# Gathering by addition: P's rows are added onto scattered Q rows in SBUF, and the identity product goes

## The reference

```python
msg_in = jnp.concatenate([x[src], x[dst], edge_attr], axis=-1)
msgs = jnp.maximum(msg_in @ mW1 + mb1, 0.0) @ mW2 + mb2
agg = jax.ops.segment_sum(msgs, dst, num_segments=num_nodes)
```

## Time and profile before

| | |
|---|---|
| median of 3 runs | 910.36 us (910.34 to 913.0) |
| the profiled execution's own time | 917.49 us |
| its span | 915.6 us |
| TensorE busy | 833.4 us (91%) |
| DVE / ACT / POOL busy | 633.4 / 506.6 / 507.5 us |
| mean granted TensorE clock | 0.968 |

### The profile page before, as it was taken

The page is one execution under the profiler, slowest core; times in us unless marked ns, Lnnn a source line. Parts: engine busy times, 40 slices in busy tenths (PEclk is TensorE's granted clock), DMA queues, the critical chain, the costliest instruction groups (busy, mean ns, idle before and its releaser), DMA issues.

```text
span 915.6 us, 18961 instructions
## 1 busy us (share of the span) xinstructions
PE 833.4 (91%) x6949; PEld 777.7 (85%) x6949; DVE 633.4 (69%) x1769; ACT 506.6 (55%) x1006; POOL 507.5 (55%) x495
## 2 busy tenths in 40 slices
PE   5448888798999989999999998999999999999996
PEld 4348878798998989998899998978899888898886
DVE  7449999688798887897978888548742311127663
ACT  5226656575786777786777876634344011114864
POOL 8577777777777777777777777661210000005110
PEclk9769999999999999999999999999999999999999
DMA  6524545867565655565555655482147777686501
GB/s 175 165 80 130 155 157 170 151 200 240 170 206 161 190 167 173 166 204 177 180 172 164 206 179 169 148 258 84 45 180 306 293 298 291 239 293 203 155 24 28
DMA packets 104976, 163.68 MB, mean 179 GB/s; under 512 B 14698, under 2 KB 65425, under 8 KB 104878
## 3 DMA queue, kind: packets, MB, share of 16 engines
q1 hardware_dynamic: 91230, 134.19, 44.5%
q0 software_dynamic: 13648, 28.21, 12.1%
HBM read 107.92 MB, written 54.43 MB: 177 GB/s over the span
## 4 chain that ended last, share of the span: by engine, by line
PE 43%; POOL 37%; issue 11%; DMA 4%; DVE 3%; ACT 1%; SPq 1%; DVEq 0%; POOLq 0%
POOL room L816 36%; PE ps L1971 14%; PE ps L1956 13%; PE ps L1796 3%; DMA room<-p_rows,idx 2%; PE ps L1797 2%; PE ps L1810 2%; PE ps L1940 2%; PE ps L1827 2%; PE ps L1829 2%; PE ps L1731 1%; POOL pair L816 1%; DMA ST<-in_src 0%; ACT h L917 0%; DVE nb L1213 0%
## 5 line engine op out<-in xcount | busy, mean ns | idle before, releaser
L816 POOL DMA_INDIRECT room<-p_rows,idx x416 | 426.5, 1025 | 132.7 <-issue 125.6
L1796 PE MATMUL ps<-room,ident 128*128 128x128 f32 x832 | 175.0, 294 | 49.0 <-DMA room<-p_rows,idx 48.2
L1796 PEld LDWEIGHTS ps<-room,ident 128*128 128x128 f32 x832 | 131.8, 200 | 52.7 <-DMA room<-p_rows,idx 41.7
L1797 PE MATMUL ps<-room 128*128 128x128 f32 x832 | 168.2, 286 | 0.0
L1331 DVE TENSOR_TENSOR room<-room,Wp 128x800 bf16<-128x800 bf16 x294 | 159.2, 570 | 3.4
L1827 PE MATMUL ps<-room 128*128 128x200 bf16 x784 | 159.0, 255 | 0.0
L1829 PE MATMUL ps<-room 128*128 128x100 bf16 x1568 | 158.2, 209 | 0.0
L1829 PEld LDWEIGHTS ps<-room 128*128 128x128 bf16 x1568 | 145.5, 98 | 4.1
L1971 PE MATMUL ps<-room,h 128*128 128x256 f32 (+1 forms) x650 | 133.5, 367 | 0.0
L1797 PEld LDWEIGHTS ps<-room 128*128 128x128 f32 x832 | 133.3, 202 | 0.0
L961 ACT ACTIVATE g<-ps 128x512 f32<-128x512 f32 x104 | 62.1, 598 | 123.1 <-PE ps L1797 123.1
(11 more groups left out here) (195 smaller groups left out, 1077.4 us busy)
## 6 DMA issues: line engine op xcount, KB each, us to landing
weight_blocks<-room SPq DMA_DIRECT2D x49, 800.0 KB
room<-weight_blocks SPq DMA_DIRECT2D x11, 3200.0 KB
room<-dst_row SPq DMA_DIRECT2D x52, 256.0 KB
count_blocks<-room SPq DMA_DIRECT2D x49, 200.0 KB
room<-count_blocks SPq DMA_DIRECT2D x6, 1600.0 KB
room<-p_rows,idx POOLq DMA_INDIRECT x416
first_c<-count_blocks SPq DMA_DIRECT2D x4, 1600.0 KB, 10.6
room<-weight_blocks SPq DMA_DIRECT2D x2, 2000.0 KB
```

Source lines behind the costliest of these rows:

```text
L816: return pool.indirect_dma_start(to, None, table, bass.IndirectOffsetOnAxis(ap=at, axis=axis))
L1796: pe.matmul(to, ident[:, :], G[:, n % GS, c, :], start=True, stop=False)
L1797: last = pe.matmul(to, sT[:, n % TS, 128 * c:128 * c + 128], Qr[:, n % QS, :], start=False, stop=True)
```

## The change

P's rows no longer pass through TensorE, from the fourth quad on:
- `pre(n)` makes only sT times Qr for n >= PLAIN = 3. A new ACT step `base(n)` copies that bank to the quad's place in one ring of RING_G = 9 quads (the six places of `G` and the three of `R`, through `rows_of`).
- The four gathers of quad n wait for `base(n)` and then add P's rows onto that place in SBUF (`rows_added`, with `compute_op=ALU.add`). `relu(n)` waits for the four gathers and works in place, SBUF to SBUF; `seg(n)` reads the same place. Quads 0 to 2 go the old way.
- `pre` and `base` run four quads ahead of `seg` (AHEAD = 4). LEAD, the lead of Q's product, goes from 4 to 6, and SP loads the one-hot rows three quads further ahead.
- `base(n)` waits until `seg(n-9)` has left the place, and TensorE waits for `base(n-2)` before it writes the bank again.
- Prologue: DVE does all variances and scales first and the conversions after them; TensorE transposes `src` after the loop over the chunks, not within it; SP stores `dst_row` and `edges_in_order` after P, and the latter after the first `rows_of_two`; POOL fills all of `sT` with ones in place of ACT.
- POOL's second widening waits for `s_seg` of the last quad in place of `s_pre`.

```diff
-        LEAD = 4
+        RING_G = GS + RS
+        LEAD = 6
+        PLAIN, AHEAD = 3, 4
...
+        def rows_of(n):
+            k = n % RING_G
+            return G[:, k, :, :] if k < GS else R[:, k - GS, :, :]
+
+        def summed_until(q):
+            return min(NQ - 1, 1 if q == 0 else q + AHEAD)
+
+        def summed_in(q):
+            return range(summed_until(q - 1) + 1 if q else 1, summed_until(q) + 1)
...
             for q in range(NQ):
-                if q % 2 == 1 and q + TS < NQ:
-                    sp.wait_ge(s_pre, q + 1)
-                    sp.wait_ge(s_sT, q + 1)
-                    rows_of_two(q - 1 + TS)
+                for m in ((4, 6, 8) if q == 1 else (q + 7,) if q % 2 == 1 and q + 7 < NQ else ()):
+                    sp.wait_ge(s_pre, m - TS + 2)
+                    sp.wait_ge(s_sT, m - TS + 2)
+                    rows_of_two(m)
...
+            pool.memset(sT[:, :, :], 1.0).then_inc(s_ones, 1)
...
+            def rows_added(to, table, at):
+                return pool.indirect_dma_start(to, None, table, bass.IndirectOffsetOnAxis(ap=at, axis=0),
+                                               compute_op=ALU.add)
...
             for q in range(NQ):
-                if q >= GS:
-                    pool.wait_ge(s_pre, q - GS + 1)
+                if q >= PLAIN:
+                    pool.wait_ge(s_base, q - PLAIN + 1)
+                gather = rows_at if q < PLAIN else rows_added
                 for c in range(4):
-                    rows_at(G[:, q % GS, c, :], P_tab, idx[:, q, c:c + 1]).then_inc(s_gat[q % GS], 16)
+                    gather(rows_of(q)[:, c, :], P_tab, idx[:, q, c:c + 1]).then_inc(s_gat[q % RING_G], 16)
...
             def relu(q):
+                if q < PLAIN:
+                    act.wait_ge(s_pre, q + 1)
+                    of = bank(q % 2).rearrange("p (c d) -> p c d", d=D)
+                else:
+                    act.wait_ge(s_gat[q % RING_G], 64 * (q // RING_G + 1))
+                    of = rows_of(q)
+                act.activation(rows_of(q), of, ACT.Relu).then_inc(s_R, 1)
+
+            def base(q):
                 act.wait_ge(s_pre, q + 1)
-                if q >= RS:
-                    act.wait_ge(s_seg, q - RS + 1)
-                act.activation(R[:, q % RS, :, :], bank(q % 2).rearrange("p (c d) -> p c d", d=D), ACT.Relu)\
-                    .then_inc(s_R, 1)
+                if q == PLAIN:
+                    act.wait_ge(s_pt, 16 * NC)
+                if q >= RING_G:
+                    act.wait_ge(s_seg, q - RING_G + 1)
+                act.activation(rows_of(q), bank(q % 2).rearrange("p (c d) -> p c d", d=D), ACT.Copy).then_inc(s_base, 1)
...
+                else:
+                    for n in summed_in(q):
+                        base(n)
+                    if q + 1 < NQ:
+                        relu(q + 1)
+                    for n in summed_in(q + 1):
+                        window_rows(n)
...
                 for c in range(4):
                     to = bank(n % 2)[:, 128 * c:128 * c + 128]
-                    pe.matmul(to, ident[:, :], G[:, n % GS, c, :], start=True, stop=False)
-                    last = pe.matmul(to, sT[:, n % TS, 128 * c:128 * c + 128], Qr[:, n % QS, :], start=False, stop=True)
+                    if n < PLAIN:
+                        pe.matmul(to, ident[:, :], G[:, n, c, :], start=True, stop=False)
+                    last = pe.matmul(to, sT[:, n % TS, 128 * c:128 * c + 128], Qr[:, n % QS, :], start=n >= PLAIN, stop=True)
```

More of the change, by code:

```diff
@@ L291, in q_bank @@
         def q_bank(n):
-            at = 256 if 2 <= n < LEAD else 128
+            at = 128 + 128 * (n // 2 if n < LEAD else 0)
             return bank(2 + n % 2)[:, at:at + 128]
@@ L355, in gnn_kernel @@
         s_pt = sem("p_rows_stored")
-        s_gat = [sem(f"gathered_{k}") for k in range(GS)]
+        s_gat = [sem(f"gathered_{k}") for k in range(RING_G)]
         s_row = [sem(f"dst_spread_{k}") for k in range(TS // 2)]
@@ L365, in gnn_kernel @@
         s_pre = sem("messages_in_psum")
+        s_base = sem("Q_rows_in_ring")
         s_R = sem("messages_ready")
@@ L588, in _ @@
                              P_row(j)[:, 0:width(j)].rearrange("p (t d) -> p t d", d=D)).then_inc(s_pt, 16)
-                if j == NC - 2:
-                    sp.wait_ge(s_dr, 2)
-                    sp.dma_start(dst_row, dst_b).then_inc(s_drs, 16)
             sp.wait_ge(s_eap, 1)
             sp.dma_start(ea_rows.rearrange("i (q e) -> q i e", e=QE), ea_r).then_inc(s_eas, 16)
[L595 to L599, removed]
+            sp.wait_ge(s_dr, 2)
+            sp.dma_start(dst_row, dst_b).then_inc(s_drs, 16)
             def rows_of_two(q):
@@ L621, in _ @@
                 rows_of_two(q)
+            sp.wait_ge(s_pk, 2)
+            for q0, q1 in ((0, QA), (QA, NQ)):
+                sp.dma_start(win_tab[2 * q0:2 * q1, :].rearrange("(q j) c -> q (j c)", j=2), pw_i[q0:q1, 0:2 * QE])\
+                    .then_inc(s_pst, 16)
+            sp.dma_start(win_tab[2 * NQ:2 * NQ + 1, 0:2 * (HALO - QE)], pw_i[NQ - 1:NQ, 2 * QE:2 * HALO]).then_inc(s_pst, 16)
             sp.wait_ge(s_pt, 16 * NC)
@@ L843, in _ @@
             widen_group(1, 0)
-            pool.wait_ge(s_pre, NQ)
+            pool.wait_ge(s_seg, NQ)
             widen_group(1, 1)
@@ L938, in store_P_again @@
                               to.rearrange("p (t d) -> p t d", d=D)).then_inc(s_pt, 16)
[L940 to L943, removed]
             for j in range(3):
@@ L951, in _ @@
                     read_P(j - 1)
-                if j == NC - 2:
-                    act.wait_ge(s_dr, 1)
-                    act.activation(dst_b, dst_r, ACT.Copy).then_inc(s_dr, 1)
             read_P(NC - 1)
+            act.wait_ge(s_dr, 1)
+            act.activation(dst_b, dst_r, ACT.Copy).then_inc(s_dr, 1)
             def relu(q):
-                act.wait_ge(s_pre, q + 1)
-                if q >= RS:
-                    act.wait_ge(s_seg, q - RS + 1)
-                act.activation(R[:, q % RS, :, :], bank(q % 2).rearrange("p (c d) -> p c d", d=D), ACT.Relu)\
-                    .then_inc(s_R, 1)
+                if q < PLAIN:
[6 more added lines that the diff above has]
+            def base(q):
+                act.wait_ge(s_pre, q + 1)
+                if q == PLAIN:
[3 more added lines that the diff above has]
+                act.activation(rows_of(q), bank(q % 2).rearrange("p (c d) -> p c d", d=D), ACT.Copy).then_inc(s_base, 1)
             def rows_off(q):
@@ L1047, in _ @@
             for q in range(NQ):
[L1048 to L1051, removed]
+                if q == 0:
+                    relu(1)
+                    window_rows(2)
+                    rows_off(3)
+                    window_rows(3)
+                elif q == 1:
+                    relu(2)
+                    base(3)
+                    for n in range(4, 6):
+                        rows_off(n)
+                        window_rows(n)
+                    for n in range(4, 6):
+                        base(n)
+                    rows_off(6)
+                    window_rows(6)
+                else:
+                    for n in summed_in(q):
+                        base(n)
+                    if q + 1 < NQ:
+                        relu(q + 1)
+                    for n in summed_in(q + 1):
+                        window_rows(n)
                 if q == 1:
@@ L1058, in _ @@
                     read_blocks(u, 0)
-                if q + 3 < NQ:
-                    rows_off(q + 3)
+                if q and summed_until(q + 1) + 1 < NQ and len(summed_in(q + 1)):
+                    rows_off(summed_until(q + 1) + 1)
                 if q - 1 in SLOT:
@@ L1220, in norm @@
                 return stage
+            for j in range(NC):
+                dve.wait_ge(*x_of(j))
+                variance(0, 0, x)(j)
+                if j:
+                    norm(0, 0)(j - 1)
+            norm(0, 0)(NC - 1)
+            dve.wait_ge(s_src, 48)
+            dve.tensor_copy(src_f, src_l).then_inc(s_srcf, 1)
+            dve.wait_ge(s_dst, 48)
+            link(dve.tensor_copy(dst_f, dst_l))
             dve.wait_ge(s_con, 2)
@@ L1227, in _ @@
             link(dve.tensor_scalar(sq[:, :], sq[:, :], -47.0, 0.0, ALU.add, ALU.max))
[L1228 to L1246, removed]
+            dve.tensor_scalar(dst_r, dst_f[:, 0:QE], sq[0:NQ, 0:1], None, ALU.subtract).then_inc(s_dr, 1)
+            dve.wait_ge(s_srcf, 1)
+            dve.scalar_tensor_tensor(pw_i.rearrange("p (e f) -> p e f", f=2)[:, :, 0], dst_f, 4096.0, src_f,
+                                     ALU.mult, ALU.add).then_inc(s_pk, 1)
             def edges_by_column(n, b, to):
@@ L1774, in _ @@
                     make_P(j - 1)
-                if j == 4:
-                    edges(2, src_f, s_srcf)
+            edges(2, src_f, s_srcf)
             make_P(NC - 1)
@@ L1787, in pre @@
                     pe.wait_ge(s_q125, 48)
-                pe.wait_ge(s_gat[n % GS], 64 * (n // GS + 1))
```

(15 more changed lines are left out.)

## The result

The changed kernel takes 1171.44 us (median of 4 runs, 1168.18 to 1179.01); the kernel before took 911.68 beside it. The ratio is 1.283, with a 95% interval of 1.278 to 1.287: slower by 28%. The forecast of 1000 us had the direction and the place, not the size, and the time lies 21 us outside the range. The profiled execution took 1174.3 us, against 917.49 before: 257 us more.

A forecast was written before the change was run, and what follows sets the result against it. POOL, issuing gathers without pause, was taken as the bound, TensorE close behind. From the profiled 917.5 us, -1.4 (prologue), -5 (sweep's end) and +97 (adding gathers) gave 1008.1, times 0.992 1000 us; range 902 to 1150.

The forecast's parts named there:

- POOL sets the pace of the sweep: Sweep: POOL issues gathers without standing still, 5.31 us a quad; TensorE, at 4.51 us a step, is second.
- The 101 x 0.88 us taken from TensorE: Sweep's body: four identity products fewer in 101 quads, step 4.51 to 3.63 us, no gain beside POOL's 5.31.
- ACT's copy and POOL's new wait cost nothing: Sweep: ACT goes to about 4.35 of 5.31 us a quad; POOL's gathers wait for `base` at no cost.
- the slack of 9.6 us: Sweep: `base(n)` is ready after 11.6 us, while POOL comes back for quad n after 21.2 us.
- An adding gather costs 0.24 us more: 404 gathers on POOL: middle between 0 and +0.47 us each, 97 us in all.
- 0.47 as its upper end: Adding gather on POOL: +0.47 us if the whole 0.947 us went by accesses, three in place of two.
- the doubling: Rival, gathers on POOL: the whole instruction doubles, +0.947 us each, 1284 us; over 0.5 us more had chance 0.13.
- The prologue gives 1.4 us: Before the sweep: P's last store and the first gather come 1.4 us sooner, bounds 0 to -2.
- The end of the sweep gives 5 us: After the last gather: last `seg` at 594.6 in place of 602.35; -5 us taken, bounds 0 and -8.
- The free gather: Rival, gathers on POOL: adding costs no more than copying, only the sweep's ends count, 904 us; chance 0.27.
- The transfers did double: Rival, gathers' DMA queue: transfers become the bound only from three times their price, 1015 us at four; chance 0.10 with clock.
- The clock did fall: Rival, TensorE in the sweep: at 1.2 GHz its step is 7.3 us, likely 20 to 60 us over; chance 0.10 with DMA.

The follow-up runs named there:

- the copying kernel: Changed kernel with its gathers copying P's rows instead of adding them, all else left: 918.04 us, ratio 1.003; with each sT times Qr product made twice, 916.45 us.

## Why the prediction was wrong

- **POOL sets the pace of the sweep, so its price per gather is the whole question:** right. 258 us more between the first and the last gather, with POOL still never idle, are the loss.
- **The 101 x 0.88 us taken from TensorE are worth nothing in the body:** right. In the copying kernel 918.04 without and 916.45 with as many products as before. In the changed one TensorE has 256 idle us from 80 to 800 us.
- **ACT's copy and POOL's new wait cost nothing:** right in the changed kernel (1.2 us of waiting). At the old pace the slack of 9.6 us was too generous: the copying kernel's POOL waits 3.7 us for ACT. It ends 0.3% over before, for which these waits are at most a part of the cause.
- **An adding gather costs 0.24 us more:** this is the term that failed. It is 0.603 us by the medians and 0.642 by the means, so 259 us in place of 97. With that term and no gain at the end the sum is 1008.1 + 162 + 5 = 1175 us, and the profiled execution took 1174.3. The fault lies in the model and not in the choice within it: I let the price go by accesses, three in place of two, and so had 0.47 as its upper end. But nine tenths of the plain gather (0.846 of 0.940) go by no rows at all, and by rows alone the addition adds 0.16 us; the other 0.45 is a surcharge on the instruction as such, which no count of rows or accesses gives. The true value lay between my 0.47 and the doubling, in a region that I gave 0.13 only because nothing seemed to lead there.
- **The prologue gives 1.4 us:** the first gather starts 1.44 us sooner. In the time alone it can't be told from nothing (0.9989, 0.9967 to 1.0011).
- **The end of the sweep gives 5 us:** not seen. The last `seg` does come 4.8 us sooner after the last gather, but in the changed kernel nothing of it is left at the end (326.1 against 325.9 us), and over all kernels the old end takes 321.3 to 325.9 us and the new one 323.0 to 326.1. I had followed it only to the last piece, and not through the load of the counts and DVE's widening on which the chain of the changed kernel goes on. What takes the gain up stays open.
- **The rivals.** The free gather and the doubled one are both excluded, 0 and 0.947 against 0.60. The transfers did double: the queue takes 19.5% of 1172.5 = 229 us an engine against 111. "Collectives: The Full Stack" of the Trainium skill, with its two source reads for an addition, agrees with that ratio of 2.06, not with POOL's instruction, which went to 1.64 times. It hides, since DMA stands at 0.53 in the sweep. The clock did fall, 0.84 granted from 80 to 800 us against 0.98 in the earlier trace rows, and costs nothing there, with TensorE idle a third of the time. But TensorE's busy time for a quad is 464.04 / (365 / 4) = 5.1 us in that stretch and not the 3.7 of the forecast: with half of `pre` gone and the lower clock it is no shorter than before (437.75 / (354 / 4) = 4.9).
- **Small sums.** The lower bounds of 906 and 902 us do not come out of their terms: (917.5 - 10 + 8) x 0.992 is 908, and (917.5 - 10) x 0.992 is 900. Neither bears on the verdict.

## What to carry to other kernels

When one engine issues all the gathers, count instructions first: here a copying gather of 64 or 128 rows costs 0.30 us of gap and some 0.85 us fixed, an adding one of 32 to 128 rows 0.30 and 1.25 to 1.29, whatever it brings, and no work taken off another engine pays for that. A fused addition is cheap only if the engine that issues it has time to spare; here 0.61 us more of POOL, which sets the pace, replaced 0.22 us of TensorE, which does not. Where an operation has no row in the trace, a fixed surcharge belongs among the bounds beside the price per row.

## What the runs showed of the hardware that I had not expected

- An indirect gather's time on POOL is nearly fixed: 0.893 us for 64 rows of 512 bytes, 0.940 for 128, and 0.946 for 128 rows of 1 KB.
- An adding gather takes 1.337, 1.421 and 1.550 us for 32, 64 and 128 rows. It makes (58896 - 13648) / 404 = 112 packets more for 128 rows: 144 in place of the copying one's 32, that is one for each row and 16. At 64 and 32 rows the same count gives 80 and 48. The fixed surcharge is not the packets': a copying gather has its 32 at 64 rows and at 128, and 16 packets more, at 32 rows, already go with 1.337 us.
- DVE work draws an indirect gather out: with none beside it, it takes 0.943 us, and beside two comparisons of two SBUF operands each in a row (fp32, then bf16) 1.433. Beside the fp32 one without the other it takes 1.014, and beside four fp32 comparisons with a scalar and the bf16 one 0.977 (copying gathers, means).
